# A merged attention and expert loop: a separate order of its stages for each engine, and the ScalarE table loads requested by name

## What is computed

```python
# first block: q is the normed x, k and v are the context
ig, fg = x3 @ Wi + bi, x3 @ Wf + bf
log_f_cum = cumsum(log_sigmoid(fg))
log_D = lower_triangle(log_f_cum_i - log_f_cum_j) + ig_j
D = exp(log_D - max_log_D)
C = (q @ k.T / 8) * D
h = C / (maximum(abs(C.sum(-1)), exp(-max_log_D)) + 1e-6) @ v
x = x + tanh(g_xattn) * per_head_norm(h) * ln_scale
# second block, n is the normed x
w, e = top_2(softmax(n @ router_w.T))
routed = sum over both of w * (silu(n @ gate_w[e]) * (n @ up_w[e])) @ down_w[e]
shared = (silu(n @ sg) * (n @ su)) @ sd
x = x + tanh(g_ffn) * (routed + shared)
```

## Time and profile before

| | us |
|---|---|
| median of 3 runs | 2926.34 |
| the profiled execution, its time | 2923.16 |
| its span on the core | 2921.6 |
| start of the merged loop, up to the gate product of chunk 4 | 134.81 |
| its middle, to the gate product of chunk 31 | 871.40 |
| its end, to the first product of the expert tiles | 148.27 |
| expert tiles and the rest | 1767.12 |

### The profile page before, as it was taken

How to read it: one execution, slowest core, us unless ns; L and a number is a source line. 1 busy time by engine, 2 the same in 40 slices (tenths; PEclk the granted TensorE clock), 3 DMA queues, 4 the chain that set the end, 5 groups by cost and what they waited for, 6 DMA issues and landing times.

```text
span 2921.6 us, 49266 instructions
## 1 busy us (share of the span) xinstructions
PE 2782.3 (95%) x17322; PEld 2292.0 (78%) x17323; DVE 1845.9 (63%) x2801; ACT 1016.3 (35%) x1948; POOL 996.7 (34%) x1147
## 2 busy tenths in 40 slices
PE   3799999999999986999999999999999999999999
PEld 2678778777777775888888888888888888888887
DVE  3787888788888854454455545545545546767676
ACT  4445444444444422232333433333333331111111
POOL 1333434443444324334434434434434411111111
PEclk7799999999999988999999999999999999999999
DMA  6555546545555542344444444444444327666655
GB/s 200 149 160 168 160 146 180 154 159 153 174 153 154 149 161 101 108 150 149 154 144 147 148 151 146 149 151 146 150 150 146 109 106 210 182 203 182 205 181 186
DMA packets 243471, 458.24 MB, mean 157 GB/s; under 512 B 99697, under 2 KB 131825, under 8 KB 240625
## 3 DMA queue, kind: packets, MB, share of 16 engines
q1 hardware_dynamic: 116976, 333.62, 33.7%
q0 software_dynamic: 34880, 73.10, 8.1%
q10 hardware_dynamic: 91488, 49.82, 6.3%
HBM read 358.96 MB, written 115.31 MB: 162 GB/s over the span
## 4 chain that ended last, share of the span: by engine, by line
PE 88%; DVE 5%; issue 3%; DMA 2%; ACT 1%; POOL 1%; SPq 0%; DVEq 0%; ACTq 0%; POOLq 0%
PE p_u L1629 39%; PE p_g L1615 10%; PE p_up L1615 10%; PE p_g L1026 6%; PE p_up L1026 5%; PE p_g L1041 2%; PE p_up L1041 2%; PE p_tr L963 2%; PE p_small L1112 2%; PE p_sc L1052 2%; PE p_u L1066 2%; PE p_u L1073 1%; PE p_sc L1602 1%; PE p_small L995 1%; PE p_u L1100 1%
## 5 line engine op out<-in xcount | busy, mean ns | idle before, releaser
L1629 PE MATMUL p_u<-w_hi,xt 128*128 128x512 f32 x3360 | 908.0, 392 | 2.8 <-DVE ctx_v L1511 2.8
L1629 PEld LDWEIGHTS p_u<-w_hi,xt 128*128 128x128 f32 x3360 | 627.6, 189 | 130.7 <-DVE ctx_v L1511 3.2
L1629 PE MATMUL p_u<-w_lo,xt 128*128 128x512 f32 x1680 | 520.8, 391 | 0.0
L1322 POOL DMA_INDIRECT xn<-mid_xn,idx_q x284 | 305.3, 1075 | 497.4 <-DVE lns L1494 400.7
L1629 PEld LDWEIGHTS p_u<-w_lo,xt 128*128 128x128 f32 x1680 | 314.7, 188 | 70.9 <-DVE w_lo L1460 5.6
L1483 DVE TENSOR_TENSOR ht<-p_sc,ht 128x512 fp32r<-128x512 f32 x74 | 51.0, 689 | 370.6 <-ACT ht L1398 370.6
L1460 DVE TENSOR_TENSOR w_lo<-stage,w_hi 128x1024 fp32r<-128x1024 f32 x200 | 230.1, 1217 | 79.8 <-ACT w_hi L1382 52.5
L1615 PE MATMUL p_g<-w_hi,ht 128*128 128x512 f32 x840 | 258.7, 389 | 1.9 <-DVE ht L1483 1.9
L1615 PE MATMUL p_up<-w_hi,ht 128*128 128x512 f32 x840 | 258.6, 389 | 0.0
L1443 ACT ACTIVATE th<-p_u 128x512 f32<-128x512 f32 x105 | 62.8, 598 | 545.1 <-PE p_u L1629 545.1
L1506 DVE SCALAR_TENSOR_TENSOR th<-th,p_u 128x512 f32<-128x512 f32 x105 | 72.1, 687 | 281.3 <-ACT th L1443 281.3
(11 more groups left out here) (220 smaller groups left out, 4714.1 us busy)
## 6 DMA issues: line engine op xcount, KB each, us to landing
mid_y<-uc SPq DMA_DIRECT2D x73, 512.0 KB, 2.6
stage<-mid_g_row SPq DMA_DIRECT2D x64, 512.0 KB, 5.4
stage<-in_eg SPq DMA_DIRECT2D x16, 2048.0 KB, 8.4
stage<-in_eu SPq DMA_DIRECT2D x16, 2048.0 KB, 14.1
stage<-in_ed SPq DMA_DIRECT2D x16, 2048.0 KB, 18.6
mid_y<-in_x SPq DMA_DIRECT2D x34, 512.0 KB
stage<-in_x SPq DMA_DIRECT2D x32, 512.0 KB
stage<-in_ctx_t ACTq DMA_DIRECT2D x32, 512.0 KB, 9.0
```

The costliest lines, as they stand in the source:

```text
L1322: nc.gpsimd.indirect_dma_start(out=xg_parts[:, n, :], out_offset=None, in_=xn_flat, in_offset=bass.IndirectOffsetOnAxis(ap=idx_q[:, n:n + ...
L1629: mm = nc.tensor.matmul(out[:, :], a[:, k, :], w[:, k, o:o + FE], start=(k == 0 and m == 0), stop=(k == KD - 1 and m == 2))
```

## The change

`TURN`, `OFFSET` and `SHIFTED` give way to `TURNS`, with an order and offsets for each engine by itself (a word such as `A3+1` means: in turn t, stage A3 of chunk t + 1). `MOVED` holds for each engine the items that stand elsewhere at the start and the end. `schedule` takes the name of the engine. What each stage does and waits for stays, but for three things: ACT asks for its function tables by name in A3 (ahead of the wait for `absf`) and in U1 (ahead of the wait for the gate product), and SP no longer loads chunk 0 a second time where the order names it.

```diff
-    TURN = ("A2", "W1", "B0", "V1", "H1", "A3", "B2", "Y1", "E1", "P1", "A4", "E2", "A1", "B1", "W2", "Y2",
...
+    TURNS = {
...
+        "tensor": "A2 H1-4 A3 B2-1 B1-1 Y1-4 Y2-4 Y3-4 A5 N1-3 Y4-4 B3-1 N2-3 A6 G1-3 G2-3 E3-3 B4-1 G3-3 "
+             "G4-3 G5-3 G6-3 Q2+1 E4-3 K7-3 K8-3 Q3+1 B0 Z1-3",
+    }
...
+    def order_of(engine):
+
+        order = list(AHEAD)
+        names = [(word[0], int(word[1]), int(word[2:] or 0)) for word in TURNS[engine].split()]
+        for turn in range(-6, NCH + 6):
+            items = [(stage, part, turn + ahead) for stage, part, ahead in names]
+            order += [item for item in items if 0 <= item[2] < NCH and item not in AHEAD]
+        for item, before in MOVED.get(engine, ()):
+            order.remove(item)
+            order.insert(order.index(before) if before else len(order), item)
+        return order
...
         def stage_x(part, b, j):
             c = b * CPB + j
+            if turn_is_first(b, j):
+                return
...
             if part == 3:
+                nc.scalar.preload_act_table_set("natural_log_exp_and_others")
                 ge(act, absf_rdy, c + 1)
...
         def stage_u(part, b, j):
             c = b * CPB + j
+            nc.scalar.preload_act_table_set("exp_and_others")
             act.wait_ge(gu_ps, c + 1)
```

More of the change, by code:

```diff
@@ L219, in mix_part @@
              ("Q", 3, 1), ("A", 7, 0), ("X", 1, 2), ("A", 8, 0), ("A", 9, 0))
-    def offset(stage, part):
-        return SHIFTED.get(f"{stage}{part}", OFFSET[stage])
-    ORDER = list(AHEAD)
-    for turn in range(NCH + 3):
-        items = [(name[0], int(name[1:]), turn + offset(name[0], name[1:])) for name in TURN]
-        ORDER += [item for item in items if 0 <= item[2] < NCH and item not in AHEAD]
-    END = NCH - 1
-    MOVED = (((("D", 1, END), ("E", 1, END), ("E", 2, END)), ("U", 1, END - 1)),
-             ((("N", 1, END), ("N", 2, END), ("E", 3, END)), ("H", 1, END - 1)),
-             ((("E", 4, END), ("Z", 1, END)), ("Y", 3, END - 1)),
-             ((("I", 1, END),), ("G", 3, END)))
@@ L245, in schedule @@
+    def schedule(engine, stages):
+        for stage, part, c in order_of(engine):
             if stage in stages:
@@ L282, in decays_at_router @@
         return capped((CPB - 2) * b + (2, 2, 3, 4)[j], (CPB - 2) * B)
-    turned = [item for item in ORDER if f"{item[0]}{item[1]}" in ("Q2", "Q3", "N1", "N2", "H1")]
+    turned = [item for item in order_of("tensor") if f"{item[0]}{item[1]}" in ("Q2", "Q3", "N1", "N2", "H1")]
     def tr_before(stage, part, b, j):
@@ L421, in stage_p @@
                 load_scales()
-        schedule({"P": stage_p, "X": stage_x, "R": stage_r, "W": stage_w, "A": stage_a, "D": stage_d,
+        schedule("sync", {"P": stage_p, "X": stage_x, "R": stage_r, "W": stage_w, "A": stage_a, "D": stage_d,
                             "F": stage_f, "E": stage_e, "J": stage_j, "V": stage_v, "Z": stage_z})
@@ L522, in stage_i @@
                     ).then_inc(row0_in, 16)
-        schedule({"L": stage_l, "A": stage_a, "C": stage_c, "D": stage_d, "E": stage_e, "I": stage_i})
+        schedule("gpsimd", {"L": stage_l, "A": stage_a, "C": stage_c, "D": stage_d, "E": stage_e, "I": stage_i})
         ge_apart(pool, past, (counts_rdy, 1))
@@ L941, in stage_z @@
             nc.vector.tensor_scalar(starts_i[:, 1, :], starts, -1.0, None, ALU.add).then_inc(counts_rdy, 1)
-        schedule({"O": stage_o, "Z": stage_z, "W": stage_w, "L": stage_l, "Q": stage_q, "A": stage_a, "S": stage_s, "B": stage_b,
+        schedule("vector", {"O": stage_o, "Z": stage_z, "W": stage_w, "L": stage_l, "Q": stage_q, "A": stage_a, "S": stage_s, "B": stage_b,
                               "F": stage_f, "C": stage_c, "D": stage_d, "E": stage_e, "N": stage_n, "U": stage_u, "H": stage_h,
@@ L1124, in stage_z @@
                 nc.tensor.matmul(p_logit[:, 0:NE], ones[:, :], hot_acc[:, :], start=True, stop=True).then_inc(cnt_ps, 1)
-        schedule({"Z": stage_z, "Q": stage_q, "N": stage_n, "A": stage_a, "B": stage_b, "E": stage_e, "G": gate_up, "K": gate_up,
+        schedule("tensor", {"Z": stage_z, "Q": stage_q, "N": stage_n, "A": stage_a, "B": stage_b, "E": stage_e, "G": gate_up, "K": gate_up,
                             "H": stage_h, "Y": stage_y})
```

72 lines of the change are left out of this document (59 added, 13 removed), and 9 rows, old and new, of tables (TURN, TURNS).

## The result

The changed kernel takes 2988.31 us (2986.16 to 2990.31, 4 runs) where the kernel before takes 2925.91 (2924.7 to 2926.47, 4 runs): a ratio of 1.0223, with a 95% interval of 1.021 to 1.0236 (the two medians alone give 1.0213). It is 62 us slower. Of all the executions behind the times of this document one, of 5557 us, belongs to no fast state and is left out. The forecast was 2889 us, and its range ended at 2912.

What follows compares the result with a forecast made beforehand. PE sets the pace in the middle, with only 37.7 us of waits to win. Savings of 24.5 + 6 + 7 = 37.5 us off the profiled 2923.16 give 2885.7; the median is 3.2 higher: 2889 us, range 2873 to 2912.

Steps and rivals of the forecast that it cites:

- The store of xn on SP: Store ahead of A4: delays the gate rows by some 2 us, counted inside the bounds of the 9 us loss.
- these bounds: Middle, ACT late before the tanh: loss between 0 (keys do not hold C1) and 20 us (all turns with a scale).
- the chain to the tanh: ACT's work up to the tanh's table load: ends at 616.1 against 616.47, 0.4 us to spare in the turn shown.
- The mechanism of the standstill: DVE's absf stood still beside POOL's product, 2.38 instead of 0.28 us; the new order lets it meet no POOL work.
- A5's waits: PE's waits for the rows of A5 in the middle: 6.5 of 9.4 us saved.
- B0 ahead of A2: On PE in the middle, B0's scores cover A2's wait of 0.81 us in 28 turns: 22.7 us saved.
- the middle: Chunks 4 to 31, 871.40 us before: 24.5 us saved (22.7 + 6.5 + 4.3 - 9), so near 847.
- The start: Ahead of the middle, 134.81 us before: 6 us saved, from 2 lost to 12 won.
- the end: From the last xn to the first expert product: PE work moved ahead saves 7 us, from 2 to 11.
- The 9 us: Loss in the middle: keys hold C1, so ACT is late before the tanh by 1.3 us in 7 turns.
- The slower case: Rival: POOL's mask also holds C1, exponentials start 5.5 us later instead of 3.2, 48 us lost: 2937 us; chance 0.06.
- The rival of DVE as the bound: D1 ahead of U1 waits for the power on POOL, 0.6 us a turn, 17 us off the middle: 2906; chance 0.15.

Runs made afterwards that it cites:

- E4: Stage of the ranks and posi; its run: changed kernel with E4 ahead of D1 on DVE, nothing else put back: 2935.04 us, ratio 1.0052.
- the old order: Kernel before with B0 ahead of A2 on PE and D1 ahead of U1 on DVE: 2933.27 us, ratio 1.0052; DVE waits 72.7 us for the power.

## Why the prediction was wrong

**The store of xn on SP.** This is the step that failed first: "The store of xn ahead of A4 on SP delays the gate rows by one issue and its traffic, some 2 us, while POOL's mask would wait for the keys anyway; I count it inside these bounds." Three things in it were wrong. The delay is 5 us and not 2: the first load of the row is issued 18.2 us behind A2 with the store ahead and 13.1 with it behind (medians; the landing is 6.4 and 2.7, and 1.4 in the kernel before). The mask does not wait for the keys: POOL has them done at 603.06 in the turn shown, and the mask starts at 608.36, behind the row. And the forecast itself gave the chain to the tanh 0.4 us to spare, so a delay of the row had nothing to take it up; 2 us in each of the 21 turns with a scale would be 42, and the bounds were 0 to 20. It costs 56 us. By the runs it is mostly not traffic (18) but SP's wait for xn, in order, ahead of a row that is ready (38), which puts the row later against POOL's scatters; neither the wait nor the scatters were in the forecast. Together with E4 behind D1 and the moved context load, both below, it makes up the whole distance: the result is 99 us above the forecast, and the three steps put back are worth 105.

**The mechanism of the standstill, seen and then lost.** The forecast read from the earlier trace rows that a small operation of DVE with two SBUF inputs stands still beside POOL's product, and that the new order takes `absf` out of its way. That came true: `absf` takes 0.28 us at the median now, and A5's waits are gone. It did not ask which operation stands there instead. POOL's product follows D1 at once, and the next operations of DVE behind D1 are those of E4. `posi` is on PE's path, since A2 waits for it. The place cost 50 us by itself. A small part of that is not the standstill: in the seven turns of j = 0 DVE also waits for the power ahead of D1, 2 to 8 us, with E4 behind it, and PE's waits for `posi` in these turns are 4.8 of the 42.3 us. The Trainium skill (SBUF — State Buffer, Who interferes with whom) says that a DVE instruction with at most one SBUF input does not contend with GpSimd outside its two-port modes, and one with two does where GpSimd's instruction reads SBUF; the turn shown agrees with both, 0.19 us for the reduction and 2.00 us for `posi` beside the same product.

**The moved context load.** A1 went from behind B2 to behind B3, and its DMA with it. The forecast had no term for it; it is worth 39 us alone and 17 us (0.9922 to 0.9865) where the other two are put back. Nor did it have one for POOL's scatters in E4.

**B0 ahead of A2.** The forecast said "DVE takes the bias directly behind U1, so I count nothing". Alone the step gives nothing, because 15.2 us come back at A3. Only with D1 ahead of U1, and C1 and C2 early, is there a gain; in the changed order all of these are there, and of 22.7 us of waits at A2 6.8 are left with the three steps put back, so 15.9 went and not 22.7.

**The rest, and some luck.** With the three steps put back, the middle is 846.50 us (forecast "near 847"), A5 waits 2.1 instead of 9.4 us (forecast 6.5 saved, 7.3 measured), A6 0.7 instead of 4.3, waits for ACT and `th` together 10.9 us (forecast 9 lost). The start is 3.7 us shorter (forecast 6) and the end 7.9 (forecast 7). That the middle comes out to the microsecond is luck. The 24.5 us of the forecast were all waits; of the 24.9 measured, 17.6 are waits (37.7 to 20.1), and 7.4 are shorter busy time of the same matmuls (833.72 to 826.36), for which the forecast had no term. The 9 us have another cause than the forecast's, too. The keys do hold C1, its first operation by 1.6 us in most turns of j = 2 and 3, and its last by 0.6 in those of j = 1. But the exponentials start behind the mask and its row, not behind C1's squares: ACT waits for the mask ahead of them for 26.8 us in 19 turns, even in this kernel.

**The rivals.** The slower case had the right place, the exponentials start too late, with a wrong cause: the mask beside C1. Such a standstill exists. In the changed kernel it stands in the turn of chunk 28, where the mask comes early, and C1's last product takes 2.60 us instead of 1.22:

```profile
988.35 2.14 POOL L517 TENSOR_SCALAR_AFFINE_SELECT stage<-stage 128x1024 f32<-128x1024 f32 x2
988.98 2.60 DVE L861 SCALAR_TENSOR_TENSOR uc<-mu,uc 128x1024 f32<-128x1024 f32 x1
```

But of the 27 turns only this one and that of chunk 4 have it; in the others the row is so late that C1 has ended when the mask starts. The rival of DVE as the bound, where D1 ahead of U1 waits for the power, is at most a small part of what happened: 34.5 us of DVE's waits in 8 turns lie there after the change, and 6.5 with the store and E4 put back, while PE waits for `th` 8.0 us in 3 turns. It does happen in the old order (72.7 us).

## What to carry to other kernels

When a table of orders changes, list for each queue what stands ahead of a small transfer now: also what its issuing engine waits for before it gets there, since that wait is paid by all behind it. When a standstill between two engines is cured by moving one operation, look at which operation the other one meets in its new place, and whether anyone on the critical engine waits for that. A saving at one wait is only one if the next wait behind it has slack of its own: B0 ahead of A2 alone took away 22.7 us of waits and 0 us of time.

## What the runs showed of the hardware

The median gate row of 8 KB lands 1.4 us behind its issue in the kernel before, and also with the store of 512 KB ahead of it (1.5). In the new orders it takes 2.7 us with the store behind it, and 5.1 when it is issued 0.8 us later, with no store ahead of it, behind POOL's scatters; the two rows of that kernel with no scatter near land in 1.4 us.

A DVE operation with two inputs in SBUF stands still until POOL's instruction has ended: `posi` takes 2.00 us instead of 0.16 beside the product, and C1's last product 2.60 instead of 1.22 beside the mask, while a reduction of one input keeps its 0.19 us beside the product.

PE's matmuls ran at a lower mean clock where PE waited more (1.00 is 2.4 GHz, 0.50 is 1.2 GHz): the same 7972 matmuls are busy 833.72 us at a mean granted clock of 1.00, with 37.7 us of waits, and 858.14 us at 0.96 with 89.8 us. From before to after, 52 us more of waits came with 24 us more of busy time, about half as much again. That is one pair of kernels and no rate: at a clock of 1.00 the busy time is 826.36 us with the three steps put back and 838.92 with B0 alone first.
